# First-stage ScalarE order, statistics of four tiles, score turns by transposes, and two low parts on VectorE, in a sequence layer with a routed feed-forward

## The reference, cut to what matters

```
x0   = layernorm(x)                                   # eps 1e-5
xln  = ln(ln(x0, ln1), tm)                            # eps 1e-12 inside
mix  = xln * time_first + shift(xln) * (1 - time_first)
r    = sigmoid(mix @ Wr)
vmix = sum_t (xln @ Wv)[t] * exp(time_decay * (T-1-t))
x2   = x0 + r * (vmix @ Wo + bo)
xc   = ln(ln(x2, ln2), cm)
x    = x + x2 + sigmoid(xc @ Wcr) * (square(relu(shift(xc) @ Wck)) @ Wcv)
```

```
h      = layernorm(x)
scores = sigmoid(h @ gate_w)                          # 2048 x 32
top 2 of 4 groups, then top 4 of the 32 experts -> combine weights
routed = sum over the 4 experts of weight * (relu2(h @ Wu[e]) @ Wd[e])
shared = relu2(h @ Wsu) @ Wsd                         # inner size 1024
out    = x + routed + shared
```

## Time and profile before

| | us |
|---|---|
| runs without a profile | 1066.85 median of 3 (1066.0 to 1069.85) |
| the profiled execution | 1070.02 |
| its span, first to last instruction | 1068.3 |
| mean granted TensorE clock | 0.994 |

### The profile page before, as it was taken

One profiled execution on the slowest core, in us unless ns is written; L12 is line 12 of the kernel. 1 busy time (PEld: TensorE's weight loads), 2 busy tenths in 40 slices (PEclk: granted clock), 3 DMA queues, 4 the chain that ended last, 5 costly groups with the idle time before them and its releaser, 6 DMA issues.

```text
span 1068.3 us, 18034 instructions
## 1 busy us (share of the span) xinstructions
PE 1039.5 (97%) x5390; PEld 855.0 (80%) x5390; DVE 635.9 (60%) x1184; ACT 549.8 (51%) x929; POOL 434.2 (41%) x328
## 2 busy tenths in 40 slices
PE   5999999999999999999999999999999999999988
PEld 2556888888888888888878888889999998889866
DVE  7967947904580467041016797957777776767604
ACT  5863546333333333323345434357777776767732
POOL 1021303221122112211224433468778787888652
PEclk8999999999999999999999999999999999999989
DMA  8605296516421642334267591168987899687766
GB/s 287 227 1 197 88 336 208 176 60 243 156 95 60 248 154 89 107 130 154 86 215 241 207 310 40 43 183 176 263 203 203 232 234 317 110 182 147 96 215 273
DMA packets 97605, 186.66 MB, mean 175 GB/s; under 512 B 15496, under 2 KB 34952, under 8 KB 97168
## 3 DMA queue, kind: packets, MB, share of 16 engines
q1 hardware_dynamic: 78304, 150.58, 40.6%
q0 software_dynamic: 18816, 34.64, 17.0%
q10 hardware_dynamic: 432, 0.79, 0.3%
HBM read 137.78 MB, written 58.98 MB: 184 GB/s over the span
## 4 chain that ended last, share of the span: by engine, by line
PE 76%; DMA 8%; issue 6%; POOL 4%; DVE 2%; ACT 2%; POOLq 0%; SPq 0%; ACTq 0%; DVEq 0%
PE bank L673 35%; PE bank L997 24%; PE bank L1614 7%; PE bank L578 5%; DMA res_d<-yo,idy 4%; PE bank L1604 2%; POOL res_d L1812 2%; DMA hTb<-hT_d 1%; POOL xg L1791 1%; POOL shx_d L1812 1%; DMA f<-in_L_attn_x 1%; PE bank L1008 1%; DMA xg<-h_d,idc 1%; PE bank L1018 1%; PE bank L1067 1%
## 5 line engine op out<-in xcount | busy, mean ns | idle before, releaser
L978 POOL TENSOR_TENSOR ksp_lo<-ra,ksp_hi 128x512 fp32r<-128x512 f32 x96 | 142.3, 1483 | 444.2 <-ACT ksp_hi L928 444.1
L1614 PEld LDWEIGHTS bank<-xT,wus 128*128 128x128 f32 x1344 | 162.8, 191 | 7.1
L1614 PE MATMUL bank<-xT,wus 128*128 128x128 f32 x1344 | 163.5, 275 | 0.0
L997 PE MATMUL bank<-vring,ksp_hi 128*128 128x512 f32 x512 | 159.4, 393 | 0.0
L920 ACT ACTIVATE ra<-bank 128x512 f32<-128x512 f32 x96 | 57.5, 599 | 180.4 <-PE bank L673 170.1
L673 PE MATMUL bank<-wd_hi,aT 128*128 128x512 f32 x336 | 126.0, 416 | 6.4 <-DVE aT L1750 3.9
L1756 DVE TENSOR_TENSOR wd_lo<-w,wd_hi 128x1024 fp32r<-128x1024 f32 x84 | 103.0, 1226 | 43.7 <-ACT wd_hi L1686 29.8
L928 ACT ACTIVATE ksp_hi<-ra 128x512 fp32r<-128x512 f32 x96 | 60.8, 634 | 122.3 <-PE bank L997 121.8
L997 PEld LDWEIGHTS bank<-vring,ksp_hi 128*128 128x128 f32 x512 | 95.5, 188 | 20.1
L673 PE MATMUL bank<-xcT_hi,wck_lo 128*128 128x512 f32 x256 | 101.7, 397 | 0.0
L673 PE MATMUL bank<-xcT_lo,wck_hi 128*128 128x512 f32 x256 | 101.5, 397 | 0.0
(11 more groups left out here) (284 smaller groups left out, 2041.2 us busy)
## 6 DMA issues: line engine op xcount, KB each, us to landing
vring<-wcv_d SPq DMA_DIRECT2D x64, 512.0 KB, 3.3
w<-in_L_ffn_Wu SPq DMA_DIRECT2D x32, 512.0 KB
w<-in_L_ffn_Wd SPq DMA_DIRECT2D x32, 512.0 KB
hT_d<-hT SPq DMA_DIRECT2D x16, 512.0 KB, 4.0
hTb<-hT_d SPq DMA_DIRECT2D x3, 2048.0 KB
raw_wcv<-in_L_attn_Wcv SPq DMA_DIRECT2D x4, 1024.0 KB, 6.9
raw_wck<-in_L_attn_Wck SPq DMA_DIRECT2D x4, 1024.0 KB, 9.5
f<-in_L_attn_x SPq DMA_DIRECT2D x4, 1024.0 KB, 7.0
```

The source lines that it names most:

```text
L978: nc.gpsimd.tensor_tensor(ksp[1][:, i % 2], ra[:, i % 2], ksp[0][:, i % 2], ALU.subtract).then_inc(sem("klo_in"), 1)
L997: m = nc.tensor.matmul(bank[to + j][:], ksp[l][:, i % 2, j * P:(j + 1) * P], rhs(r), start=i == 0 and k == 0, stop=i == last and k == 2)
L1614: m = nc.tensor.matmul(bank[4 + u][:, n * P:(n + 1) * P], wus[u][:, c * EI + n * P:c * EI + (n + 1) * P], xT4[:, u, c * P:(c + 1) * P], st ...
```

## The change

Five edits. (1) `act_stats` is also used for set 4 (tiles 12 to 15), and VectorE drops its bn_stats for them; three semaphores of that function become one. `dve_params` runs in the middle of set 5 and not of set 4. (2) ScalarE's list in stage 1 is in a new order: two decays come before the first statistics, the other early ones behind the first normalisation; three of the four long exponentials, the last decays, two normalisations and the high parts of two weights trade places. (3) Tile 1 of x is loaded by ScalarE's DMA queue, ahead of the gain and bias rows, and TensorE runs 12 idle matmuls and not 10. (4) The logits are turned by four transposes of 64 rows; ScalarE copies the 256 columns, GpSimd adds the two halves (`pool_logits`), and ScalarE takes the sigmoid one step later. `pair` is gone, and `pe_counts` stands behind step 2 and not step 1. (5) In stage 5 the low parts of steps 0 and 1 are made by VectorE at the end of stage 4, and GpSimd starts with step 2.

```diff
-        BY_ACT = (2, 3)
+        BY_ACT = (2, 3, 4)
...
-                dve.wait_ge(sem("asq_in"), a0 + 4)
+                dve.wait_ge(sem("astat_in"), 5 * (a0 // 2 + 2))
...
-            for g in range(4):
+            for g in range(5):
                 dve_set(dve, st, g)
-            dve_set(dve, st, 4, middle=lambda: dve_params(dve, st))
-            dve_set(dve, st, 5)
+            dve_set(dve, st, 5, middle=lambda: dve_params(dve, st))
...
         def stage1_scalar(act):
+            act.dma_start(f1_flat[:, 1:2], x_pairs[0][:, 1:2]).then_inc(sem("x1_in"), 16)
             for n, v in enumerate(("ln1_g", "ln1_b")):
                 act.dma_start(g1b[:, n], vec(f"L0_attn_{v}")).then_inc(sem("g1_in"), 16)
             act.dma_start(tdb[:], vec("L0_attn_time_decay")).then_inc(sem("tdb_in"), 16)
-            act_stats(act, 0, 4)
             act.wait_ge(sem("ages_in"), 2)
             act.wait_ge(sem("tdb_in"), 16)
             for t in range(2):
                 act_decay(act, t)
+            act_stats(act, 0, 4)
             act_stats(act, 2, 6)
-            for t in range(2, 4):
-                act_decay(act, t)
             act_norm(act, 0)
-            for t in range(4, 8):
+            for t in range(2, 8):
                 act_decay(act, t)
...
             for t in range(8, 12):
                 act_decay(act, t)
+            act_stats(act, 8, 12)
+            act_stats(act, 10, 14)
+            act_norm(act, 3)
             for c in range(1, C):
                 act_dsum(c)
-            act_norm(act, 3)
-            act_hi(act, "wr")
             for t in range(12, NT):
                 act_decay(act, t)
-            act_hi(act, "wcv0")
+            act_norm(act, 4)
+            act_hi(act, "wr")
             for c in range(C):
                 act_shifted(act, 0, c)
-            act_norm(act, 4)
+            act_hi(act, "wcv0")
...
-            pe_idle(pe, 10)
+            pe_idle(pe, 12)
...
             if i == TH_AT + 2:
                 wait_apart(act, sem("tsc_in"), b + 1)
-                nc.scalar.activation(scores[:, bass.ds(b * BT, BT)].rearrange("p j e -> p (j e)"), bank[6][:, 0:BT * E],
-                                     ACT.Sigmoid).then_inc(sem("sc_in"), 1)
+                nc.scalar.activation(lsum[:].rearrange("p j s e -> p (j s e)"), bank[6][:, 0:BT * 2 * E], ACT.Copy).then_inc(sem("lslo_in"), 1)
+            if i == TH_AT + 3:
+                wait_apart(act, sem("lsum_in"), b + 1)
+                nc.scalar.activation(scores[:, bass.ds(b * BT, BT)], lsum[:, :, 0], ACT.Sigmoid).then_inc(sem("sc_in"), 1)
...
+        def pool_logits(pool, b):
+            wait_apart(pool, sem("lslo_in"), b + 1)
+            nc.gpsimd.tensor_tensor(lsum[:, :, 0], lsum[:, :, 0], lsum[:, :, 1], ALU.add).then_inc(sem("lsum_in"), 1)
...
-                m = nc.tensor.matmul(bank[6][:, j * E:(j + 1) * E], lgT[:, j * P:(j + 1) * P], pair[:], start=True, stop=True)
+                m = nc.tensor.transpose(bank[6][:, j * 2 * E:(j + 1) * 2 * E], lgT[:, j * P:(j + 1) * P],
+                                        ident[0:2 * E, 0:2 * E])
...
-            pe_block3(pe, 1, between={1: pe_counts})
+            pe_block3(pe, 1, between={2: pe_counts})
...
             a_lo(rest + GROUP - 1, 1)
+            for i in range(2):
+                dve.wait_ge(sem("khi_in"), N4 + i + 1)
+                nc.vector.tensor_tensor(ksp[1][:, i % 2], ra[:, i % 2], ksp[0][:, i % 2],
+                                        ALU.subtract).then_inc(sem("klo_in"), 1)
...
-                    if last and k == GROUP - 1:
-                        pool_inner(pool, N4, 0)
...
-            for i in range(1, NSI):
+            pool.wait_ge(sem("klo_in"), 2 + N4 + 2)
+            for i in range(2, NSI):
                 pool_inner(pool, N4 + i, i)
```

More of the change, by code:

```diff
@@ L149, in program @@
         bna0, bna1 = (at(name, [P, 4, 2], F, 185.125 + n / 4) for n, name in enumerate(("bna0", "bna1")))
-        asum = at("asum", [P, 3, 8], F, 185.5)
+        asum = at("asum", [P, 3, 12], F, 185.5)
         vring = at("vring", [P, 4, 2 * H], R, 80)
@@ L166, in program @@
         lgT = at("lgT", [2 * E, BLK], F, 182)
-        pair = at("pair", [2 * E, E], F, 184.25)
+        lsum = at("lsum", [P, BT, 2, E], F, 184.25)
         tmp = at("tmp", [P, BT, H], F, 186)
@@ L431, in act_stats @@
             act.wait_ge(sem(f"part_in{tile // 2}"), 16)
+            done = 5 * (a0 // 2)
             for k in range(2):
                 nc.scalar.activation(unused[:, 0:H], xt(tile + k), ACT.Copy,
-                                     accum_out=asum[:, 0, a0 + k:a0 + k + 1]).then_inc(sem("asum_in"), 1)
-                act.wait_ge(sem("asum_in"), a0 + k + 1)
-            nc.scalar.activation(asum[:, 1, a0:a0 + 2], asum[:, 0, a0:a0 + 2], ACT.Copy, scale=-1.0 / H).then_inc(sem("amean_in"), 1)
-            act.wait_ge(sem("amean_in"), a0 // 2 + 1)
+                                     accum_out=asum[:, 0, a0 + k:a0 + k + 1]).then_inc(sem("astat_in"), 1)
+                act.wait_ge(sem("astat_in"), done + k + 1)
+            nc.scalar.activation(asum[:, 1, a0:a0 + 2], asum[:, 0, a0:a0 + 2], ACT.Copy, scale=-1.0 / H).then_inc(sem("astat_in"), 1)
+            act.wait_ge(sem("astat_in"), done + 3)
             for k in range(2):
                 nc.scalar.activation(unused[:, 0:H], xt(tile + k), ACT.Square, bias=asum[:, 1, a0 + k:a0 + k + 1],
-                                     accum_out=asum[:, 2, a0 + k:a0 + k + 1]).then_inc(sem("asq_in"), 1)
-                act.wait_ge(sem("asq_in"), a0 + k + 1)
+                                     accum_out=asum[:, 2, a0 + k:a0 + k + 1]).then_inc(sem("astat_in"), 1)
+                act.wait_ge(sem("astat_in"), done + 4 + k)
         def act_norm(act, g):
@@ L713, in stage1_sync @@
         def stage1_sync(sp):
-            for j in range(2):
-                sp.dma_start(f1_flat[:, j:j + 1], x_pairs[0][:, j:j + 1]).then_inc(sem(("part_in0", "x1_in")[j]), 16)
+            sp.dma_start(f1_flat[:, 0:1], x_pairs[0][:, 0:1]).then_inc(sem("part_in0"), 16)
             sp_x(sp, 1)
@@ L865, in stage2_vector @@
             nc.vector.tensor_tensor(gw[:, :, 1], gwf[:], gw[:, :, 0], ALU.subtract).then_inc(sem("gwlo"), 1)
-            nc.vector.tensor_tensor(pair[:], ident[0:2 * E, 0:E], ident[0:2 * E, E:2 * E], ALU.add).then_inc(sem("gwlo"), 1)
             for j in range(BT):
@@ L981, in stage2_gpsimd @@
         def stage2_gpsimd(pool):
-            with pool.Fori(0, NB) as b:
+            for i in range(NCI):
+                pool_inner(pool, i, i)
+            with pool.Fori(1, NB) as b:
                 for i in range(NCI):
                     pool_inner(pool, b * NCI + i, i)
+                    if i == TH_AT + 2:
+                        pool_logits(pool, b - 1)
         def pe_inner_up(pe, n, i, weights, rhs, kc=4):
@@ L1103, in stage2_tensor @@
             pe_block2(pe, 0, first=True)
-            pe.wait_ge(sem("gwlo"), 2)
+            pe.wait_ge(sem("gwlo"), 1)
             with pe.Fori(1, NB - 1) as b:
@@ L1288, in pool_block3 @@
                 if first and i == TH_AT + 2:
+                    pool_logits(pool, NB - 1)
                     pool_numbers(pool)
```

## The result

The changed kernel takes 1061.93 us (median of 6 runs, 1060.23 to 1062.76) where the kernel before took 1068.22 beside it (6 runs, 1066.0 to 1069.85): a ratio of 0.994 [0.9925, 0.9954], 6.3 us or 0.6% faster. The forecast was 1057.4, within 1054 to 1063; its own row had 1055.5 to 1059. Two more groups of runs gave 1060.47 against 1066.6 and 1063.08 against 1070.48: 6.1 and 7.4 us.

What follows compares the result with a forecast made beforehand. TensorE, with three quarters of the span, was taken as the bound. First stage 0, scores -2.3, routing 0 and last block -7.15 sum to -9.45: 1060.6 us profiled, 1057.4 as a median, range 1054 to 1063.

Steps and rivals of the forecast that it cites:

- its own row: Whole kernel: the forecast case itself among the listed chances, 1055.5 to 1059 us, chance 0.44.
- First stage: Start to the end of the first turn: net change 0 us, bounds -1 to +1.5.
- the start wins 5 us and the end of the stage loses them: First stage: TensorE's lead of about 5 us is lost to ScalarE's statistics and the late dwb, net 0.
- Two decays now stand in that wait: First stage, ScalarE's wait until 11.36: holds two decays, 1.3 us; first normalisation starts at 18.1 to 18.3.
- the waits of 1.0 and 1.5 us ahead of tiles 4 and 8: First stage: TensorE waits 1.0 us for ScalarE's third normalisation, then 1.5 us behind the late VectorE.
- Rival A: First stage: waits drop the clock, tile 10 on at half speed, 3.2 us lost, time 1060.6; chance 0.27.
- Scores: Four score turns: transposes replace a matmul pair, 0.57 us saved each, 2.3 us in all.
- Routing: Routing runs 6.3 us later but hidden behind an existing wait: cost 0, bounds 0 to 1.5 us.
- cover: VectorE's 7.78 us wait before the third one-hot absorbs the later routing; 1.5 us of it left.
- wait for ids: Routing: a wait for ids near 659 would show the forecast wrong.
- Last block: VectorE's low parts remove the gap (4.93 us) and clock loss (2.22): -7.15 us, bounds -7.2 to -4.9.
- the last stores meeting the DMA traffic: Kernel's end: the last four tiles' stores just miss the DMA traffic, 0 to 1 us lost.

Runs made afterwards that it cites:

- before: Profiled execution of the kernel before the change, no edit: 1070.02 us.
- b1: The kernel before, profiled once more without an edit: 1070.57 us, ratio to its own other runs 1.0004.
- e2: Changed kernel with the last block's first two low parts back on GpSimd: 1070.87 us, ratio 1.001 to the kernel before.
- e5: Changed kernel with the 12 idle matmuls at the start replaced by 100 fp32 transposes: 1060.91 us, ratio 0.9938 to the kernel before.
- a1: The changed kernel profiled again without an edit: 1060.47 us, ratio 0.9935 to the kernel before.
- e3: Changed kernel with the pair matrix and its matmul back for the scores, counts one step earlier: 1066.59 us, ratio 0.9964 to the kernel before.
- e1: Changed kernel with the whole first-stage edit undone: 1063.1 us, ratio 0.9931 to the kernel before.
- e4: Changed kernel with the first turn's fourth chunk moved behind tile 10's decayed sum: 1059.94 us, ratio 0.9916 to the kernel before.
- e8: Changed kernel keeping only the start of the first-stage edit, last four tiles' statistics back on VectorE: 1061.0 us, ratio 0.9913 to the kernel before.
- e7: Changed kernel with both the fourth chunk behind tile 10 and the rest add cut in four: 1058.71 us, ratio 0.9914 to the kernel before.
- e9: Changed kernel with only the start of the first-stage edit kept and the rest add cut in four: 1061.88 us, ratio 0.9915 to the kernel before.
- after: First profiled execution of the changed kernel, no further edit: 1060.23 us.
- a2: The changed kernel profiled a third time without an edit: 1063.08 us, ratio 0.9925 to the kernel before.
- e6: Changed kernel with VectorE's 128x2048 rest add in the last block cut into four of 128x512: 1062.12 us, ratio 0.9948 to the kernel before.

## Why the prediction was right, and where not

Per part, from the means of the marks: first stage +2.0 (79.45 for six against 77.48 for three), scores -1.9, routing +0.1, last block -6.5 (43.0 for eight against 49.6 for before, b1 and e2). The sum is -6.3, and the medians say -6.3, -6.1 and -7.4. The forecast was -9.45. The time, 1061.93, lies inside 1054 to 1063 and outside the forecast's own 1055.5 to 1059. Of the 4.5 us between it and 1057.4, 3.1 are these parts; 1.4 are the kernel before, whose median was 1066.85 in three runs and 1068.22 in six.

- **First stage, 0 predicted, +2.0 measured, outside its bounds of -1 to +1.5: the term that failed.** The working said "the start wins 5 us and the end of the stage loses them". In the profiled execution the end was as written: dwb at 63.79 (64.15 forecast), a wait of 2.49 (2.9), the next products from 64.50 (64.6). The start was not, for two reasons. The bullet "Two decays now stand in that wait" took ScalarE's wait as one for tiles 4 and 5, to 11.36 us; the decay vector, issued fourth on that queue, landed at 11.1 to 12.7 in the eleven executions with this queue, and the table load behind it added 1.28. And the idle matmuls, put 0.4 us later, started at 8.5 to 9.9 in these eleven, against 6.6 to 6.8 in the three with the old queue: 2.1 us later in the profiled one, over at 21.5 and not 19.5. The first tile came at 21.53, not 19 to 20. It won the clock (3.0 us) and no start, and the waits of 1.0 and 1.5 us ahead of tiles 4 and 8 were 0 and 0.34.
- **What the 2.0 us are.** Not the late start: e5 starts its tiles 1.4 us behind a1 and reaches the second turn 0.1 behind it. The end of the stage hangs on ScalarE's list, which now begins with the decay vector: in the six executions the vector lands at 11.13 to 11.88, and the last chunk of the turn starts 52.86 to 52.93 us behind it each time. The profiled execution had the earliest landing. In a1, e2 and e3 the 32 records start at 65.12 on average, 0.5 behind the forecast; the clock adds 0.6 on average. And the sum was made against a late execution of the kernel before: its 16 records took 10.06 us where b1 has 9.59 and e1, with the same list, 8.83, so its second turn was at 78.00 and the mean of the three is 77.48, another 0.5. The rest are 0.2 that its own sum had and left out (64.6 against 64.43) and 0.2 between two readings of the old turn's end (64.43, next products from 64.26). No run lands the vector earlier, so what that would give isn't shown.
- **Rival A** happened in half the executions, at 1.2 us (80.04 against 78.85) and not 3.2: the clock was back after 4 us. It was priced from tiles 0 and 1, which follow a gap of 4.21 us. It needs the wait: the seven executions without one in the turn, e4 and e8 among them, keep 1.00 there, and e5 shows that transposes without a gap raise and keep the clock. Whether transposes beside a wait make a fall likelier than matmuls would isn't shown.
- **Scores, -2.3 predicted.** Each turn saves 0.62 (0.57 forecast); three of them are seen, -1.9.
- **Routing, 0 predicted, up to +0.7 measured.** Scores at 599.89 (600.2 forecast), 3.8 us of cover left (1.5 forecast), no wait for ids. But the fourth saving is gone by M3. A wait of TensorE for a low part at 651.37 (0.36 us; one like it is in all eleven profiles with transposes and in none of the three without) is the one new idle time that all of them share there; that it is the whole of it isn't shown.
- **Last block, -7.15 predicted, -6.5 measured.** Gap and clock went as written. The term was too large by the wait for GpSimd's last low part; with the cut the stretch is 42.3 us, 7.3 under before. But M5 isn't the end: the working allowed 0 to 1 us for the last stores meeting the DMA traffic, and from M5 to the end it is 5.8 us in the three with the old low parts, 6.2 in the eight, and 6.7 to 7.7 with the cut. To the end of the span the part is worth 6.1 us, cut or not within 0.4.
- **The profiled pair** agreed with -9.45 by luck: 3.7 us of its 9.8 are the routed stage, which spreads by nearly 9 us. That 1061.93 lies within 1054 to 1063 is owed to the width of that range, and not to the first stage's term.

## What to carry to other kernels

Before work is put into an engine's wait, find what ends that wait for the new work: its own input's landing, and the table load of the first activation, which is free only while something else is waited for. When statistics go to another engine, follow every product that the old engine formed behind them up to its reader; a later product can be covered by moving one tile of matmuls ahead of its reader. A faster start is worth nothing where the end of the stage hangs on another engine's list, as e5 shows. And when a gap ahead of the last results is closed, look at what the DMA engines still have to do: in e7 and e9 they, and not TensorE, were busy last. Where one stretch of a kernel spreads by more than the change is worth, compare marks around the edits and not spans.

## What the runs showed of the hardware that I had not expected

- A wait of 2.49 us in the turn was followed by a clock of 0.50 in three executions and by 1.00 in three.
- fp32 transposes bring TensorE to full speed like matmuls: 100 in 13.76 us from a cold start.
- GpSimd's 128x512 low part took 1.29 us alone and 2.2 to 3.2 us where it began during VectorE's 128x2048 add of two SBUF operands (after, a1, a2, e3, e4, e5), which kept its 2.29 us. In e1 the low part began first (1052.10, 1.30 us) and the add took 3.07. In e6 the add was cut and the low part took 1.34 us in its midst, and the four adds 3.59. So the one that begins later is longer by about what is left of the other's instruction: in the first profile of the changed kernel the add had 1.51 us left, and the low part took 1.36 more than alone. The Trainium skill (SBUF — State Buffer, SBUF: two separate sides) says that the two engines share a pair of ports, that whichever starts first has it for its whole instruction, and that the other is blocked; the times agree with it, and the runs show only the times.
- The routed stage, the same code in all, took from 310.8 to 319.6 us, on one chip 311.0 and 318.0.
